# A GRU with a feed-forward layer behind it: the initial state's load cut in four, one turning of x and the weight rounding moved one step up, fewer warming matmuls

## The reference

```python
def cell(h, x):
    gi = x @ W_ih + b_ih
    gh = h @ W_hh + b_hh
    i_r, i_z, i_n = jnp.split(gi, 3, axis=-1)
    h_r, h_z, h_n = jnp.split(gh, 3, axis=-1)
    r = sigmoid(i_r + h_r); z = sigmoid(i_z + h_z)
    n = tanh(i_n + r * h_n)
    return (1.0 - z) * n + z * h

# xt: all hidden states, (1024, 256); E = 128 experts, K = 8 bases of I = 128, TOPK = 4
probs = softmax(xt @ w_router); topk_p, topk_idx = top_k(probs, 4)
basis = silu((xt @ w_gate).reshape(T, K, I)) * (xt @ w_up).reshape(T, K, I)
mixed = einsum('tek,tki->tei', mix[topk_idx], basis)        # mix from the amplitudes
out = einsum('teh,te->th', einsum('tei,ih->teh', mixed, w_down), topk_w * expert_scale[topk_idx])
out = out + (silu(xt @ shared_w_gate) * (xt @ shared_w_up)) @ shared_w_down
x = x + out
```

## Time and profile before

| | us |
|---|---|
| median of 3 runs | 148.21 (148.15 to 151.74) |
| profiled execution, its own time | 147.87 |
| its span, first to last instruction | 146.0 |
| TensorE busy | 136.3 |
| VectorE busy | 111.6 |
| ScalarE busy | 68.1 |
| GpSimd busy | 68.9 |

### The profile page before, as it was taken

The page is one execution under the profiler, slowest core; times in us unless marked ns, Lnnn a source line. Parts: engine busy times, 40 slices in busy tenths (PEclk is TensorE's granted clock), DMA queues, the critical chain, the costliest instruction groups (busy, mean ns, idle before and its releaser), DMA issues.

```text
span 146.0 us, 4048 instructions
## 1 busy us (share of the span) xinstructions
PE 136.3 (93%) x1494; PEld 98.0 (67%) x1494; DVE 111.6 (76%) x411; ACT 68.1 (47%) x222; POOL 68.9 (47%) x123
## 2 busy tenths in 40 slices
PE   7997999999679989999999999999999998899981
PEld 5565767766347658766876687668766875597881
DVE  2215588998967997898789878987898789949661
ACT  1204638565557345535553555255526541522830
POOL 2201115667754893466147614751475148566030
PEclk9999999999999999999999999999999999999999
DMA  3898970000000000010001000100010000000102
GB/s 97 270 369 288 343 235 5 7 0 2 0 0 4 0 0 4 4 36 4 0 0 40 0 0 0 43 0 0 7 36 0 4 7 31 0 0 0 36 4 72
DMA packets 5799, 7.12 MB, mean 49 GB/s; under 512 B 916, under 2 KB 4244, under 8 KB 5780
## 3 DMA queue, kind: packets, MB, share of 16 engines
q1 hardware_dynamic: 5472, 6.70, 13.7%
q10 hardware_dynamic: 308, 0.17, 0.4%
HBM read 5.81 MB, written 1.05 MB: 47 GB/s over the span
## 4 chain that ended last, share of the span: by engine, by line
PE 51%; DVE 34%; ACT 7%; issue 3%; POOL 1%; DVEq 0%
PE unit L604 18%; PE gates L595 11%; DVE sc_out L851 7%; PE down L674 6%; ACT sc_add L412 4%; DVE keys L934 4%; PE gates L559 4%; PE turned L744 3%; DVE pre L842 3%; DVE hT L858 3%; DVE m L839 2%; DVE p L899 2%; DVE wlo L871 2%; PE unit L574 2%; ACT trz L405 2%
## 5 line engine op out<-in xcount | busy, mean ns | idle before, releaser
L299 POOL CAST hThi<-hT 128x64 fp32r<-128x64 f32 x32 | 11.1, 347 | 54.5 <-DVE hT L858 54.1
L604 PE MATMUL unit<-whi,hThi 128*128 128x512 f32 x80 | 33.7, 421 | 2.7 <-POOL wlo L334 2.0
L604 PE MATMUL unit<-wlo,hThi 128*128 128x512 f32 x80 | 31.6, 395 | 0.0
L604 PE MATMUL unit<-whi,hTlo 128*128 128x512 f32 x80 | 31.6, 394 | 0.0
L405 ACT ACTIVATE trz<-gates 128x128 f32<-128x128 f32 x32 | 8.9, 277 | 43.8 <-PE gates L595 43.8
L595 PE MATMUL gates<-whh,hT 128*32 128x192 f32 x512 | 27.4, 332 | 1.7 <-DVE hT L858 1.1
L595 PEld LDWEIGHTS gates<-whh,hT 128*32 128x32 f32 x512 | 13.5, 109 | 12.7 <-DVE hT L858 5.6
L851 DVE TENSOR_TENSOR_SCAN sc_out<-sc_mul,sc_add 128x128 f32<-128x128 f32 x32 | 15.3, 479 | 8.0 <-ACT sc_add L412 7.7
L604 PEld LDWEIGHTS unit<-whi,hThi 128*128 128x128 f32 x80 | 15.1, 188 | 8.7 <-issue 3.5
L604 PEld LDWEIGHTS unit<-whi,hTlo 128*128 128x128 f32 x80 | 15.0, 188 | 3.5
L412 ACT ACTIVATE sc_add<-pre 128x64 f32<-128x64 f32 x32 | 10.3, 322 | 14.5 <-DVE pre L842 14.5
(11 more groups left out here) (129 smaller groups left out, 243.3 us busy)
## 6 DMA issues: line engine op xcount, KB each, us to landing
wraw<-in_L_ffn_w_gate_dram SPq DMA_DIRECT2D x2, 512.0 KB, 6.0
wraw<-in_L_ffn_w_up_dram SPq DMA_DIRECT2D x2, 512.0 KB, 7.8
out_dram<-ot SPq DMA_DIRECT2D x8, 128.0 KB, 2.0
xtok<-in_x_dram SPq DMA_DIRECT2D x7, 128.0 KB, 4.1
wih<-in_L_cond_W_ih_dram SPq DMA_DIRECT2D x2, 384.0 KB, 4.3
whh<-in_L_cond_W_hh_dram SPq DMA_DIRECT2D x1, 512.0 KB, 6.5
whh<-in_L_cond_W_hh_dram SPq DMA_DIRECT2D x1, 256.0 KB, 5.8
wraw<-L_ffn_shared_w_gate_dram SPq DMA_DIRECT2D x1, 256.0 KB, 7.5
```

The costliest lines, as they stand in the source:

```text
L299: pool.tensor_copy(hThi[:, c % 3, :, :, k], hT[:, c % 2, :, k, :]).then_inc(hThi_ready, 1)
L604: last = pe.matmul(dst, st[:, p % 3, s, :, :].rearrange("p b t -> p (b t)"), w[:, s, :, cols], start=(s == 0 and n == 0), stop=(s == KB - ...
```

## The change

Five edits. h0 is loaded by four DMAs of 32 partitions each rather than by one of 128, all ahead of chunk 1 on ScalarE's queue, and VectorE waits for all four. The turning of x chunks 2 and 3 stands in step 0, and ScalarE's copy of them too. Each entry of the three tables for the weight pieces stands one step earlier. In each block of a unit the product with the low weights is the last of the three, and in the first chunk TensorE waits for the high part of the piece before the first and for its low part before the third matmul. `WARM` is 10.

```diff
-WARM = 16
+WARM = 10
-TURN_PAIR = {1: 2, 2: 4, 3: 6}
-KEEP_PAIR_SCALAR = {1: 2}
+TURN_PAIR = {0: 2, 2: 4, 3: 6}
+KEEP_PAIR_SCALAR = {0: 2}
-HI_AT = [(0, 0), (0, 0), (0, 0), (0, 2), (2, 4), (4, 6), (6, 8), (8, 10)]
-LO_VECTOR_AT = [[], [], [], [], [2], [4], [5], [8]]
-LO_POOL_AT = [[], [], [], [0], [1], [3], [6], [7], [9]]
+HI_AT = [(0, 0), (0, 0), (0, 2), (2, 4), (4, 6), (6, 8), (8, 10)]
+LO_VECTOR_AT = [[], [], [], [2], [4], [5], [8]]
+LO_POOL_AT = [[], [], [0], [1], [3], [6], [7], [9]]
...
-            act.dma_start(h0[:, :], cond.rearrange("b (j c) -> j b c", j=NJ)).then_inc(ld_h0, 16)
+            for j in range(NJ):
+                act.dma_start(h0[Q * j:Q * (j + 1), :], cond[:, FJ * j:FJ * (j + 1)]).then_inc(ld_h0, 16)
...
+            def wait_low(u, s):
+                i = PIECES.index((u, s))
+                if i in LO_VECTOR:
+                    pe.wait_ge(w_lo, LO_VECTOR.index(i) + 2)
+                else:
+                    pe.wait_ge(w_lo_pool, LO_POOL.index(i) + 1)
+
-            def three(dst, p, cols, blocks):
+            def three(dst, p, u, blocks):
 
+                cols = slice(UW * u, UW * (u + 1))
                 for s in blocks:
-                    for n, (st, w) in enumerate(((hThi, whi), (hThi, wlo), (hTlo, whi))):
+                    if p == 0:
+                        pe.wait_ge(w_hi, PIECES.index((u, s)) + 2)
+                    for n, (st, w) in enumerate(((hThi, whi), (hTlo, whi), (hThi, wlo))):
+                        if p == 0 and n == 2:
+                            wait_low(u, s)
                         last = pe.matmul(dst, st[:, p % 3, s, :, :].rearrange("p b t -> p (b t)"), w[:, s, :, cols],
...
             def unit(n, blocks):
                 p = n // NU
                 u = unit_order(p)[n % NU]
-                if p == 0:
-                    for s in blocks:
-                        i = PIECES.index((u, s))
-                        if i in LO_VECTOR:
-                            pe.wait_ge(w_lo, LO_VECTOR.index(i) + 2)
-                        else:
-                            pe.wait_ge(w_lo_pool, LO_POOL.index(i) + 1)
...
-            dve.wait_ge(ld_h0, 16)
+            dve.wait_ge(ld_h0, 16 * NJ)
```

More of the change, by code:

```diff
@@ L639, in unit @@
                         pe.wait_ge(early_ready, 1 + max(i for i in range(NE // 2) if i % len(early_bank) == n))
-                last = three(unit_bank[n % NB][:, :].rearrange("p (g n) -> p g n", g=2), p,
-                             slice(UW * u, UW * (u + 1)), blocks)
+                last = three(unit_bank[n % NB][:, :].rearrange("p (g n) -> p g n", g=2), p, u, blocks)
                 if KB - 1 in blocks:
```

## The result

The changed kernel takes 149.49 us in the median of 19 runs (148.28 to 150.87), the kernel before 148.48 in the median of 19 beside it. The ratio is 1.0072, with a 95% interval of 1.0049 to 1.0094: slower by 0.7%, inside the 2% and inside the range, and 1.2 us above the 148.3 that was predicted. The profiled execution took 149.93 with a span of 148.0 (before: 147.87 and 146.0).

What follows compares the result with a forecast made beforehand. Behind step 10 the order of TensorE's own work was taken to bound the kernel. Terms +1.26 - 0.48 + 0.83 - 1.50 = +0.11 on 147.87 gave 147.98, with 0.34 for unprofiled runs 148.3 us; range 146.8 to 150.0.

Steps and rivals of the forecast that it cites:

- H0: Start of h_part of step 0: from 10.07 to 11.33 us, +1.26; wrong if moved by under 0.5 or over 2.5.
- TensorE's order bounds everything behind step 10: Behind step 10 TensorE's own work order binds, so the end moves by whatever step 10's h_part start moves.
- H10: Start of h_part of step 10, 45.15 us before, expected near 45.3; the end moves with it.
- h0 in four transfers: Start, ScalarE's queue: four issues put chunk 1's issue at 3.58 instead of 2.34, so step 0's h_part starts 1.26 us later.
- chunk 1 isn't late: Rival at the start: load spread over more engines lands within 4.1 us of issue; 147.1 us; chance 0.28.
- fewer warming matmuls: Start: six warming matmuls fewer free 1.29 us of TensorE queue, at most 0.6 usable, lost waiting for chunk 1: worth nothing.
- rival (c): Start: TensorE's clock rises later, work behind chunk 1's turning up to twice as long; 151.5 us; chance 0.08.
- Turning in step 0: Turning of x chunks 2 and 3 leaves step 1, -0.48 us, and costs nothing in step 0's idle time.
- Pieces a step sooner, steps 4 to 7: VectorE's low half ahead of m costs +0.63 us in step 4, +0.2 in step 5, 0 in 6 and 7.
- Steps 8 and 9: Weight work gone from step 8 gives -0.94 us, unit 4's wait gone from step 9 -0.56; together -1.50.
- Low product last: Units' waits: low halves are no longer late, so 0.46 us of grace for them is worth nothing: 0.
- Sum: All terms: +1.26 - 0.48 + 0.83 - 1.50 = +0.11 on the profiled 147.87, so 147.98; 148.3 expected unprofiled.

Runs made afterwards that it cites:

- experiment 2: Changed kernel with 16 warming matmuls instead of 10, h0 still in four transfers: four of 10 executions at 147.51 to 148.03 us, six at 149.96 to 150.46.
- experiment 8: Changed kernel with h0 in one transfer and 20 warming matmuls: median 147.27 us, ratio to the kernel before 0.9922.
- experiment 5: Kernel before with 10 warming matmuls instead of 16, nothing else changed: 147.51 us once, and 149.91, 150.51, 150.64.
- experiment 6: Kernel before with h0 in four transfers, nothing else changed: 149.76, 150.59, 151.63, 151.65 us; ratio 1.0177.
- experiment 1: Changed kernel with h0 in one transfer again, 10 warming matmuls: one of 10 executions 145.86 us, one 147.42, eight 148.2 to 149.8.
- experiment 7: Changed kernel with h0 in one transfer and 16 warming matmuls: 146.10, 146.42, 146.98, and 150.04, 150.41 us.
- experiment 11: As experiment 8, but VectorE's low halves in the steps of the kernel before: median 147.72 us of 12.
- experiment 9: As experiment 8, but the three tables of the weight pieces as in the kernel before: median 147.86 us of 12.
- experiment 10: As experiment 8, but the low product second again, with its wait before it: median 147.25 us of 9.
- experiment 3: Changed kernel with 16 more warming matmuls between the first x product and the turning of chunk 1: 150.06 to 151.42 us in four executions.
- experiment 4: Changed kernel with chunk 1 of x issued ahead of h0's four pieces on ScalarE's queue: 149.10 to 149.45 us in four executions.

## Why the prediction was right or wrong

The measured 149.49 lies in the range, 1.2 us above the forecast. Most terms were right; one, the clock, was put at nothing and was not nothing, and another error hid a part of it. Two of the prediction's own signs of being wrong came in the profile after: H0 moved by 3.28, more than 2.5, and h_part(0) ran at the lower level.

- **TensorE's order bounds everything behind step 10**: right. H10 later by 2.01, span longer by 2.0.
- **h0 in four transfers**: right, and nearly to size. One issue 0.39 to 0.45 (0.45 taken), chunk 1 issued at 3.50 (3.58), landing 5.5 after it (5.0), turned at 9.03 (8.9); with the clock held, H0 +1.34 (+1.26; experiment 2). Averaged over all executions it costs 0.7 to 1.3 (the table behind experiment 8). The rival "chunk 1 isn't late" is out: from issue to landing it took 5.5, not less. The Trainium skill's rule (DMA: Bandwidth & Descriptors, "Why a DMA increments its semaphore by 16 and not by 1") on how a transfer is spread may hold, but what I drew from it, a quicker landing of chunk 1, did not come; no run here shows the engines.
- **The clock, under "fewer warming matmuls"**: the term that failed. "Worth nothing" held for the 0.6 us of queue; the clock was rival (c) with a chance of 0.08 and should have been a term beside chunk 1. Against an early rise, a late one costs 2.04 us at H0 by experiment 5, and with 10 it is missed more often. But rival (c) was half of it: I let the rise be late and priced 3.2 us, and never asked how often the kernel before misses it too (36 of 87), which is why the average loses so little by this edit. In the profiled execution the clock rose in time, by 4.1, and fell as TensorE ran out of work ahead of the late chunk; that cost 1.90 behind chunk 1 and 0.34 in step 0, 2.24 in all. This fall goes with h0 in four transfers, and I had no term for it there: experiment 6 shows it with 16 warming matmuls, and by the mean granted clock (0.989 or less) it came in 7 of the 33 executions of the changed kernel and experiments 2 and 6, in 2 of 10 of experiment 1, and in none of the others, the 87 of the kernel before among them. Of the trace before, the two speeds of the warming matmuls said that the rise comes within the 16, and cutting six takes away just those around it; the third of the three times before, 151.74, was the other sign, and I passed over it. The Trainium skill's rule that activity releases the clock (TensorE: Matmul & The Clock Gate, "What's actually happening") agrees with experiments 5, 7 and 8: missed in 3 of 4 with 10, 2 of 5 with 16 and none of 8 with 20. The time of 151.5 that I gave beside it was too high.
- **Turning in step 0**: right, -0.48 in step 1 in every kernel with it, and nothing in step 0 where the clock is up (2.93 in experiment 2).
- **Pieces a step sooner, steps 4 to 7**: right place, too large: +0.34, +0.21, +0.01, +0.05 for +0.63, +0.2, 0, 0. In step 4 the half took 0.99 as predicted, but there had been some slack ahead of m, so that m came only 0.70 later after h_part (1.93 for 1.23 us); 0.15 of this came back between m and the scan (0.93 for 1.08), and 0.2 was the time by which hT had been ahead of TensorE's early pairs, which I had counted in step 5 but not here.
- **Steps 8 and 9**: right, too small in 8: -1.18 for -0.94, and -0.56 for -0.56. I gave the gain of step 8 to ScalarE's rounding, and read VectorE as waiting from 37.06 to 38.00. It did its low half from 37.02 for 0.69 and waited only the 0.28 that stands in the earlier trace rows:

```profile
37.02 0.69 DVE L871 TENSOR_TENSOR wlo<-wraw,whi 128x512 fp32r<-128x512 f32 x1
```

Experiment 11 shows that the gain comes with this half gone, since with ScalarE's and GpSimd's work alone moved only 0.11 is left. The wait of unit 3 cost step 8 nothing (experiment 9), and step 9 needed no earlier piece.

- **Low product last**: right, 0, beside the tables (experiment 10). Without them it is worth 0.55 in step 9.
- **Sum**: the steps from 1 to 9 brought 1.61 us, not 1.15; chunk 1 cost 1.38, not 1.26; the clock, left out, cost 2.24 in the profiled execution. With these the median without the clock's term would be 148.21 + 1.38 - 1.61 = 148.0, so the clock is worth about 1.5 us of the 149.49. That the number stayed in the range is in part luck: without the 0.46 that the steps gave beyond my sum it would be 149.95, at the edge of the range, 150.0.

**Open.** The runs do not tell what makes the clock rise early in one execution and at 10 us or later in another of the same kernel, nor why it fell in the changed kernel's profile and in experiment 6's but not in experiment 2's. The length of the idle time ahead of chunk 1 alone does not decide it: it fell with 0.79 us of it and with 1.83 (there after 0.08), and stayed up through 1.30.

## What to carry to other kernels

Ahead of dropping warm-up work, look at where in it the matmuls change speed, and at whether the times of the kernel fall in groups: the number that is enough in one execution need not be in the next, and four more, at a price of 0.8 us, were cheap against the 3.5 us of a missed rise. Compare the average of all executions too, and not only the early ones: by it this change is no loss. A transfer issued behind others on the same queue is as critical as the first in-order instruction that waits for it; splitting a load in four delayed the issue of the next by 1.2 us. And where work moves from a late step to an early one, ask in each step which engine ends last: the same subtraction cost 0.35 us in one step and gave 1.1 in another.

## What the runs showed of the hardware

- The clock's rise, estimated from the lengths of the matmuls, came at 3.8 to 6.6 us, or only at 10.0 to 13.3 (experiments 1, 3, 4, 5, 7) although TensorE was busy nearly all the time between, mostly with matmuls of 4 rows and of 32 columns at a time. In experiment 3 it came during a block of 16 full-array matmuls.
- The clock fell soon after TensorE ran out of work: 0.08 us after the last matmul in the changed kernel's profile, about 0.55 after it in experiment 6's, and not within 1.30 in experiment 2's. It then stayed down for 6.8 and 3.4 us, though TensorE worked again from 9.0 on.
- VectorE's low half took 0.99 to 1.14 us beside GpSimd's and 0.68 without it, and GpSimd's two halves 1.87 rather than 1.42. A single-column VectorE operation (`den`) took 0.67 when it started 0.08 behind GpSimd's subtraction (experiment 11) and 0.20 when it started 0.60 behind it.
- On ScalarE's queue a transfer of 32 rows of 256 bytes was issued in 0.39 to 0.45 us, one of 128 rows in 0.65.
